# Second feed-forward product of layer 0 with the weights standing and 512 tokens moving, and its result turned back

## The reference, cut to what matters

```python
n2 = _ln(h, g2, b2)                                              # (4, 1024, 192)
ffn = jax.nn.gelu(n2 @ W1 + bf1, approximate=False) @ W2 + bf2   # 192 -> 768 -> 192
return h + ffn
```

## Time and profile before

| | us |
|---|---|
| median of three runs | 1915.02 |
| lowest, highest | 1910.84, 1923.53 |
| the profiled execution, own time | 1911.3 |
| its span in the trace | 1909.6 |
| feed-forward stage of pair 0, in that trace | about 331 to 421 |
| feed-forward stage of pair 1, in that trace | about 1259 to 1348 |

### The profile page before, as it was taken

The page is one execution under the profiler, slowest core; times in us unless marked ns, Lnnn a source line. Parts: engine busy times, 40 slices in busy tenths (PEclk is TensorE's granted clock), DMA queues, the critical chain, the costliest instruction groups (busy, mean ns, idle before and its releaser), DMA issues.

```text
span 1909.6 us, 26407 instructions
## 1 busy us (share of the span) xinstructions
PE 1615.0 (85%) x9798; PEld 902.6 (47%) x9798; DVE 1296.8 (68%) x3017; ACT 978.4 (51%) x1393; POOL 127.7 (7%) x165
## 2 busy tenths in 40 slices
PE   0759887988999999996557898889899999999835
PEld 0357646564333333355334584656523333333814
DVE  4666674026899998946778487531489889996478
ACT  0422353214777777762732325431357777777345
POOL 6010000000000000002420100000000000000020
PEclk9977898999899999998678687989989999999957
DMA  6003220007101000000110212000430010000001
GB/s 155 1 1 116 54 62 1 1 1 210 38 30 30 26 26 26 17 1 5 30 34 0 83 51 77 21 1 1 131 109 26 26 34 26 26 26 1 1 1 34
DMA packets 53894, 73.39 MB, mean 38 GB/s; under 512 B 18712, under 2 KB 27205, under 8 KB 53767
## 3 DMA queue, kind: packets, MB, share of 16 engines
q1 hardware_dynamic: 52150, 68.54, 12.4%
q0 software_dynamic: 1616, 3.16, 0.7%
HBM read 38.51 MB, written 33.17 MB: 38 GB/s over the span
## 4 chain that ended last, share of the span: by engine, by line
PE 68%; DVE 22%; ACT 4%; issue 2%; DMA 2%; POOL 1%; SPq 1%; DVEq 0%; ACTq 0%
PE PV L906 10%; PE ST L890 9%; PE S L856 7%; PE ST L802 4%; PE ST L557 4%; PE MT L856 3%; PE PV L915 2%; DVE nmp L1545 2%; DVE st L1418 2%; PE S L813 2%; DVE amax L1653 2%; DVE R L1652 2%; PE ST L587 1%; PE S L851 1%; DVE Er L1473 1%
## 5 line engine op out<-in xcount | busy, mean ns | idle before, releaser
L1234 ACT ACTIVATE Er<-ST 128x1024 f32<-128x1024 f32 x384 | 377.1, 1021 | 105.6 <-PE ST L890 105.3
L1597 DVE TENSOR_REDUCE nmp<-S 128x1 f32<-128x512 f32 x514 | 337.4, 683 | 30.6 <-PE S L856 30.6
L890 PE MATMUL ST<-QS,KS 100*128 100x512 bf16 x768 | 218.0, 385 | 0.3
L906 PE MATMUL PV<-Er,V 128*17 128x512 f32 x1536 | 211.6, 600 | 0.0
L856 PE MATMUL S<-KS,QS 96*128 96x512 bf16 x514 | 183.4, 392 | 0.9
L1597 DVE TENSOR_REDUCE nmp<-MT 128x1 f32<-128x512 f32 x254 | 173.4, 683 | 13.5 <-PE MT L856 13.5
L856 PEld LDWEIGHTS S<-KS,QS 96*128 96x128 bf16 x514 | 48.3, 98 | 154.8 <-DVE nmp L1597 103.7
L451 POOL TENSOR_SCALAR tp<-mv 128x8 f32<-128x8 f32 x20 | 5.6, 278 | 1667.2 <-DVE mv L1422 1667.2
L1545 DVE TENSOR_REDUCE nmp<-S 128x1 f32<-128x512 f32 x120 | 77.4, 683 | 48.5 <-PE S L672 48.2
L890 PEld LDWEIGHTS ST<-QS,KS 100*128 100x128 bf16 x768 | 72.1, 99 | 64.3 <-ACT Er L1234 5.7
L856 PE MATMUL MT<-KS,QS 96*128 96x512 bf16 x254 | 99.4, 391 | 0.9 <-DVE nmp L1597 0.9
(11 more groups left out here) (387 smaller groups left out, 3079.7 us busy)
## 6 DMA issues: line engine op xcount, KB each, us to landing
KS<-scr_k SPq DMA_DIRECT2D x72, 192.0 KB, 2.7
scr_k<-R SPq DMA_DIRECT2D x16, 576.0 KB, 4.0
QS<-scr_q SPq DMA_DIRECT2D x48, 192.0 KB, 2.8
scr_k<-R SPq DMA_DIRECT2D x16, 384.0 KB, 4.6
QS<-scr_k SPq DMA_DIRECT2D x24, 192.0 KB, 2.5
scr_q<-R SPq DMA_DIRECT2D x8, 576.0 KB, 4.7
scr_k<-R SPq DMA_DIRECT2D x16, 192.0 KB, 5.2
scr_q<-R SPq DMA_DIRECT2D x8, 384.0 KB, 5.0
```

Source lines behind the costliest of these rows:

```text
L890: ins = nc.tensor.matmul(ST[i % 2][:, (kt % 2) * HALF:(kt % 2 + 1) * HALF], KS[0:KP + 4, k, kt * P:(kt + 1) * P], QS[0:KP + 4, k, half * H ...
L906: ins = nc.tensor.matmul(PV[row:row + VC, :], slots[h // H].V[:, kt, h % H, :], E[:, step % RING, (kt % 2) * HALF:(kt % 2 + 1) * HALF], st ...
L1234: A_(E[:, g, :], ST[i % 2][:, :], ACT.Exp).then_inc(s["exps"], 1)
L1597: v.tensor_reduce(nmp[:, u // 2, u % 2:u % 2 + 1], bank, AX.X, ALU.max).then_inc(s["reduced"], 1)
```

## The change

The second product now has slices of `W2` standing (128 rows by 96 channels) and 512 tokens moving (`down`), so that its result lies with channels on partitions, one chunk of 96 channels in each `o.D2` bank. ScalarE copies each bank into the used-up half of `o.XT` and adds the bias there, one value for each partition (`ycopy`). TensorE turns the result back into token tiles (`turn_back`), and VectorE's add waits for that instead. `bf2` is loaded as a column of `cols`, and the bias product is gone. On ScalarE `ycopy` of half 0 stands ahead of the slot's `gelu` of half 1. In half 1, both slots' `down` come before both slots' `turn_back`.

```diff
-            load(bf2[:], A["L0_ffn_bf2"].rearrange("(a n) -> a n", a=1))
+            load(cols[:, :, 7], A["L0_ffn_bf2"].rearrange("(c p) -> p c", p=CH))
...
-            def back(p, o, half):
+            def down(p, o, half):
+
                 pe.wait_ge(o.s["gelu"], p * 12 + FC * (half + 1))
-                for i in (2 * half, 2 * half + 1):
-                    if i >= 2:
-                        pe.wait_ge(o.s["h2"], p * 4 + i - 1)
+                if half:
+                    pe.wait_ge(o.s["h2"], p * 4 + 2)
+                for m in range(2):
+                    for f in range(FC):
+                        ins = nc.tensor.matmul(o.D2[m][0:CH, :], wf2[:, f, m * CH:(m + 1) * CH], o.hid[:, f, :], start=f == 0, stop=f == FC - 1)
+                    ins.then_inc(o.s["ffn"], 1)
+
+            def turn_back(p, o, half):
+                pe.wait_ge(o.s["ycopied"], p * 4 + 2 * half + 2)
+                for i in range(2):
                     for t in (2 * i, 2 * i + 1):
-                        d = o.D2[i % 2][:, (t % 2) * D:(t % 2 + 1) * D]
-                        for f in range(FC):
-                            nc.tensor.matmul(d, o.hid[:, f, t % HT * P:(t % HT + 1) * P], wf2[:, f, :], start=f == 0, stop=False)
-                        ins = nc.tensor.matmul(d, ones[0:1, :], bf2[:], start=False, stop=True)
-                    ins.then_inc(o.s["ffn"], 1)
+                        for m in range(2):
+                            n = half * HALF + t * P
+                            ins = nc.tensor.transpose(o.D2[i][:, (t % 2) * D + m * CH:(t % 2) * D + (m + 1) * CH], o.XT[0:CH, m, n:n + P], ident[0:CH, 0:CH])
+                    ins.then_inc(o.s["yturned"], 1)
...
                 for o in slots:
-                    back(p, o, 0)
+                    down(p, o, 0)
                     up(p, o, 1)
-                for o in slots:
-                    back(p, o, 1)
+                    turn_back(p, o, 0)
+                for o in slots:
+                    down(p, o, 1)
+                for o in slots:
+                    turn_back(p, o, 1)
...
+            def ycopy(p, o, half):
+                for m in range(2):
+                    act.wait_ge(o.s["ffn"], p * 4 + 2 * half + m + 1)
+                    A_(o.XT[0:CH, m, half * HALF:(half + 1) * HALF], o.D2[m][0:CH, :], ACT.Identity, scale=1.0, bias=cols[:, m, 7:8]).then_inc(o.s["ycopied"], 1)
+
...
-                for half in range(2):
-                    for o in slots:
-                        gelu(p, o, half)
+                for o in slots:
+                    gelu(p, o, 0)
+                for o in slots:
+                    ycopy(p, o, 0)
+                    gelu(p, o, 1)
+                for o in slots:
+                    ycopy(p, o, 1)
...
             def ffn(p, o, half):
                 for i in (2 * half, 2 * half + 1):
-                    ve.wait_ge(o.s["ffn"], p * 4 + i + 1)
+                    ve.wait_ge(o.s["yturned"], p * 4 + i + 1)
                     add(o, i, o.s["h2"])
```

More of the change, by code:

```diff
@@ L119, in build @@
         wf2 = sb("wf2", [P, FC, D])
-        bf2 = sb("bf2", [1, D])
         wat = sb("wat", [CH + 1, 2, 3 * D])
@@ L166, in build @@
         OWN = """gathered stats rstd xnorm turned evac inproj inproj_out conv silu gated proj hi resid mid lo vproj vcopied
-            hidden gelu ffn h2 bhid bgelu hss hrms hquant hturned hcopied bout outs stored kw0 kw1 qw0 qw1""".split()
+            hidden gelu ffn ycopied yturned h2 bhid bgelu hss hrms hquant hturned hcopied bout outs stored kw0 kw1 qw0 qw1""".split()
         slots = []
```

## The result

The changed kernel takes 1925.8 us in the median of 20 runs (1916.2 to 1941.3), the kernel before 1917.6 us in 20 runs beside it (1909.5 to 1924.4). The ratio is 1.0063 with a 95% interval of 1.0044 to 1.0082: 12 us slower, 8 to 16 (the means lie 11.2 us apart, the medians 8.2). The forecast was 1926 us, 11.3 us slower and within 1%.

A forecast was written before the change was run, and what follows sets the result against it. Bound by TensorE's stream and, behind it, a seam where only VectorE works. Stream +0.5 and seam +5.1 us a pair make 11.2 us for two pairs, plus 0.1 for the load: 11.3 us slower, 1926 us, range 1917 to 1939.

The forecast's parts named there:

- The stream stays level: TensorE's feed-forward products: down 1.4 us a pair shorter, turning 1.8 us longer, so the stream ends about 0.5 us later.
- the turning: Eight transposes on TensorE per turn_back: 0.11 us each, 0.9 us in all, with bounds of 0.6 and 2.2 us.
- The copy: ScalarE's evacuation of 96 x 512 with the bias: 0.77 us each, 16 of them, at no cost in half 0.
- ScalarE and VectorE in half 0 are covered: In half 0, ScalarE's copies fit its idle time and VectorE's adds, 10 us later, make nothing late: no cost.
- The seam is the loss: Behind the stream, a's adds and statistics are no longer hidden: first transpose at 9.84 us, not 4.75, 5.1 us a pair.
- The clock in the seam costs no more: Transposes behind the seam run slow for about 3.5 us after either idle length, so the longer seam costs only its length.
- The stages behind take no more: Stages after the feed-forward: the longest takes 411.5 and 411.7 us in the two pairs, so a shift does not stretch it.
- The load: At the start, the bias fetched as 192 single values between loads TensorE awaits: +0.1 us, at most half a microsecond.
- The sum: Whole kernel: 5.6 us a pair, 11.2 for two, plus 0.1 for the load: 11.3 us slower, 1926 us, within 1%.
- Rival 1: In the stream, turn_back's transposes count as idling and drop the clock: 10.8 us on top, 1937 us; chance 0.05.
- Rival 2: In down, 128 rows cost 0.05 us more per instruction than 96: 9.6 us added, 1936 us; chance 0.05.
- Rival 3: Not slower: down's products with 96 columns standing go faster, 0.37 us an instruction for a level result; chance 0.06.

The follow-up runs named there:

- e1_turn_early: The changed kernel with a's last turning put between the two channel chunks of z's last down: 1922.2 us, ratio 1.0033 to the kernel before.
- c0_before_again: The kernel before, run again with no edit as a control: 1913.6 us, ratio 0.9984 to the kernel before.
- e6_stats_spread: Kernel before, bias product replaced by VectorE adding bf2 to the residual, plus each two tiles' statistics right behind their add: 1894.1 us, ratio 0.9889 to before.

## Why the prediction was right, point by point

- *The stream stays level.* Forecast 0.5 us longer a pair, measured 0.0. `down` took 10.3 us as worked out. The term that was mis-sized is the turning: 8 x 0.11 = 0.9 us was taken, and it measured 0.66, since transposes with 96 columns moving start 0.08 us apart. The lower bound of 0.6 was the nearer one, although 128 columns are loaded. The copy was put at 0.77 us and took 0.68, hidden either way.
- *ScalarE and VectorE in half 0 are covered.* So the rows at 371.10 and 381.88 show, and the window in which TensorE is busy for 83.90 of 83.90 us. The number of table loads did not grow either.
- *The seam is the loss.* Forecast 5.1 us a pair, measured 4.68. The order of events is the forecast one, instruction for instruction; a's first add came 0.53 us behind the stream and not 0.65, and of two adds in a row the second started 0.44 to 0.48 us behind the first and not 0.59. TensorE idled 7.62 us; "about 7.5" was forecast. Both interventions agree: a's statistics moved into the old kernel's seam cost 2.61 us a pair, and a's work taken out of the new one's seam gave back 2.1. So the place of a's work is shown to be the greater part of the loss. The rest, 2.5 us a pair, was read off the timeline of e1_turn_early and not taken away by an edit.
- *The clock in the seam costs no more.* From the first transpose to the first projection it was 5.9 and 6.3 us before, and 6.7 and 6.7 in the first profile after, but 6.2 and 5.7 in the second, and 6.6 and 5.9 in the kernel before's second. No difference stands out.
- *The stages behind take no more.* This failed in a small way. The earlier trace rows gave the length of layer 1's attention, but not whether anything in it would start later. TensorE's wait for the queries, up to 1.73 us and at nothing in the sum, came on top: between the first transpose and the scores the four stages of the changed kernel took 0.9 us more on average than those of before (34.5 and 33.6).
- *The load.* 0.1 us was forecast; the start varies by 2.7 us between profiles of any kernel, so the term can't be seen, and it stays open.
- *The sum.* 11.3 us forecast, 11.3 by the traces up to the scores, 12 (8 to 16) and 9 (4 to 14) by the runs. That it agrees so closely is partly luck. Stream and seam were put 0.9 us a pair too high (5.6 for 4.68), and the wait for the queries, left out, is of that size. The forecast of 1926 us met the median of 1925.8 by chance as well: the median of the three runs on which it stood was 2.5 us under that of the twenty.
- *Rival 1 (the clock falls while TensorE turns back)* is refuted: PEclk is 1.00 over 83.9 us with two `turn_back` in it. The Trainium skill (TensorE: Matmul & The Clock Gate, Part 4: PE-mode transpose) says that the full clock does not engage for transposes; the trace does not agree.
- *Rival 2 (128 rows dearer than 96)* is refuted: 192 instructions of `down` start 0.43 us apart. What made me weigh it, 0.18 us between the instructions of `back`, was the bias product's after-effect and not the rows: without the bias they start 0.1625 us apart.
- *Rival 3 (96 columns standing are cheaper)* is refuted by the same 0.43 us.

What the prediction did not see is the better edit. It counted the bias at 8.3 us of a pair and went on; with its after-effect it was 11.2 us, and all of it could be had without turning the product round.

## What to carry to other kernels

When a product is turned round so that its result needs a copy and a turning, price the last stage before the next dependency and not only the stream: here the stream came out level to 0.1 us, and the greater part of the seams' loss was work of one slot that had been hidden beside the other's products; the rest was the way over ScalarE, and behind the seam a transfer that came later. Ask of each instruction what stood in front of it in its engine's order before and what stands there now. A bias as a product of one row can cost more than its own rows show; an idle engine adding it to the residual costs nothing.

## What the runs showed of the hardware

- **A busy TensorE can stay at 1.2 GHz.** In the changed kernel's mixing stage TensorE was busy without a gap for 25.8 us, with float32 products of 192 columns whose weight loads fill 24.37 us of it, and was granted half its clock throughout; the window of that stretch:

```profile
302.70:328.50 25.80, 25.80 (x82) 24.37 (x80) 6.61 (x24) 1.40 (x3) 1.90 (x2) 0.50 0.00 0
```

In pair 1 of c0_before_again the same code was granted the full clock after its first products: six groups of eight took 1.46 us each from 1236.15 on, and the clock fell again for the last two, behind 1.38 us idle. TensorE's idle time ahead of the stage, 2.37 us, is the same in all twenty. The Trainium skill (TensorE: Matmul & The Clock Gate, Part 1: The HAM clock gate) says that activity releases the throttle; busy time alone did not do so here. What decides it was not tried.
- **The one-row product costs its neighbours.** Two instructions of 0.26 us each made a tile 0.70 us longer, not 0.52: the step ahead of them and the second step behind them are 0.25 to 0.27 us long in place of 0.1625.
- **After 3.12 us idle the clock can be full or low.** In e6_stats_spread the four first transposes of the next norm took 0.64 us in pair 0 and 1.09 us in pair 1, after the same idle time:

```profile
416.57 0.64 PE L539 MATMUL PV<-ident,X 128*96 128x128 f32 x4 [3.12 <-DVE X L1427]
1333.00 1.09 PE L539 MATMUL PV<-ident,X 128*96 128x128 f32 x4 [3.12 <-DVE X L1427]
```

After 4.68 us and more idle it was low (1.09 us for four) in all eighteen seams of the other profiles.
